# Relative attention on one core: two key tiles in one round of TensorE's tilings, every second tile of maxima scores in full mode

## The chip, the cores and the metric

The kernel runs on one core of one Trainium2 chip. The time is device microseconds of one execution. Before the change three runs took 2206.95, 2209.48 and 2213.20 us; the median is 2209.48 us.

## The reference, cut to what matters

Two layers run over x of shape (2, 1024, 128): attention with rotary positions, a mixture of 8 experts, attention with biases, and a last block of relative attention and 32 experts. The change lies in the relative attention, with 16 heads of 8 columns in each of two batches, so 32 heads in all:

```python
q, k, v = x @ wq, x @ wk, x @ wv                 # 16 heads of 8
p = (pe @ wp).reshape(2 * Ss - 1, H, HD)         # projected relative positions
ac = jnp.einsum('bihd,bjhd->bhij', q, k)
bd_full = jnp.einsum('bihd,phd->bhip', q, p)
rel = jnp.arange(Ss)[:, None] - jnp.arange(Ss)[None, :] + (Ss - 1)
bd = bd_full[:, :, jnp.arange(Ss)[:, None], rel]
att = jax.nn.softmax((ac + bd) * scale, axis=-1)
attn_out = jnp.einsum('bhij,bjhd->bihd', att, v).reshape(Bs, Ss, Ds) @ wo
```

## The kernel before, in words

**A score** is a sum of two products. The content term has 8 columns, split in high and low parts to keep float32 precision: three products stacked on 32 partitions, the *stack* (Qs, Ks). It takes a quarter of TensorE's rows, and Qs and Ks hold it four times, on partitions 0, 32, 64 and 96, so that four of its matmuls can run beside each other ("row stage", `32*128` in the profile). The position term is a full product over 128 partitions: A, made of q and the projected positions, times a fixed table E, each again in high and low parts (Ah, Al in Ahs and Als, Eh, El).

**Two passes per head.** The first finds each query's maximum: for each of 8 query tiles, the stack and Ah x Eh are added in banks 2 and 3 (`stack_scores` L692, `scores` L700), and VectorE takes the negative maximum over 1024 keys (L1144) into M. `max_row` (L733) turns M's 8 columns into rows, ScalarE copies them (L1413), and SP writes them into a row of the stack on two of its four copies (L376), so that the second pass subtracts the maximum. The second pass makes the scores turned, keys on partitions: for each of 8 key tiles kt, the stack (`stack_turned`, L709) and three full products for each half of the queries (`turned`, L715) in banks 0, 1 or 4, 5, in turn; ScalarE takes the exponential (L1426) into PR; `values` (L725) adds PR times V in bank 6, four matmuls in column mode (`128*32`), two passes each. ScalarE copies bank 6 out (L1409).

**A position** is one turn over a head n. Its eight rounds carry the second pass of head n beside the first pass of head n + 2 and the preparation of A of head n + 3 (`prep`, L683: a stack matmul with the weights Ws, in bank 7; VectorE multiplies it by a table, L1139; GpSimd adds, L1622; ScalarE and GpSimd split it in high and low, L1418, L1624). The instructions of each engine stand in the order written by hand; an engine takes them one after the other, and a wait for a semaphore holds back all behind it. Heads 1 to 28 run in a loop of four positions per turn; the heads 0 and 29 to 31 are written out. Ahead of head 0 stands a start, in which the maxima of heads 0 and 1 and the preparations of 0 to 2 are made.

**Slots.** Qs, Ks, Ws, Ahs, Als and M have four slots, head n in slot n mod 4. So head n + 3 goes into the slot of head n - 1. SP, at position n, waits until all 16 halves of turned scores of head n - 1 are done (`st_done`), then issues nine loads for head n + 3: four of Qs and four of Ks (L362), one of Ws (L367). `prep(n + 3, ..., 0)` waits for them (`qk_in`, `ws_in`):

```python
def position(n, s, ahead):                      # SP
    if ahead:
        e.wait_ge(st_done, 1 + 16 * (HB + n))
        load(n + 3, (s + 3) % SLOTS)
    store(n - 1, (s - 1) % SLOTS)
    max_rows(n + 1, (s + 1) % SLOTS)
```

In a round before, TensorE has three parts: row stage (two stack matmuls of the turned scores, two of the maxima scores, in rounds 2 to 5 a preparation), full part (two maxima scores, six turned), values in column mode.

Of the kernel before, what the change touches and what calls it, by code (L numbers as in the profile page):

```python
# [87 lines left out]
def two_layers(nc, A, out):  # L88
    with ExitStack() as ctx:
# [30 lines left out]
        XT = sb("XT", [P, TT * P])  # L120
# [5 lines left out]
        cols = sb("cols", [P, 8])  # L126
# [13 lines left out]
        Ws, Ws_r = two("Ws", [KR, SLOTS, 2 * P])  # L140
# [5 lines left out]
        El = sb("El", [P, L], F32R)  # L146

# [149 lines left out]
        def _(e):  # L297
# [67 lines left out]
            def load_rel(n, s):  # L365
                load_qk(n, s)
                e.dma_start(Ws_r[:, s, :].bitcast(F32), w_stack[bass.ds(n, 1)].rearrange("n r t -> (n r) t")).then_inc(ws_in[s], 16)  # L367
# [150 lines left out]
        def _(e):  # L518
# [153 lines left out]
            def relative_attention():  # L672
                HB = 2 * NH

                def prep(n, s, p, block):

                    if p == 0:
                        e.wait_ge(qk_in[s], 128 * (2 * NH // SLOTS + block + 1))
                        e.wait_ge(ws_in[s], 16 * (block + 1))
                    if p == 0 and not (isinstance(n, int) and n < 3):  # L680
                        e.wait_ge(mt_copied, HB + n - 1)
                    e.wait_ge(prep_mul, 4 * n + p)
                    e.matmul(bank(7), Ws_r[:, s, (p % 2) * P:(p % 2 + 1) * P],  # L683
                             Qs_r[0:KR, s, (p // 2) * GW:(p // 2 + 1) * GW], start=True, stop=True)\
                        .then_inc(prep_ps, 1)

                def stack_scores(n, s, qt, bk=2):

                    e.wait_ge(max_done, 2 + 8 * (HB + n) + qt - (2 if isinstance(n, int) and n < 2 else 0))
                    for kh in range(2):  # L690
                        rows_ = slice((2 + kh) * KR, (3 + kh) * KR)
                        e.matmul(bank(bk + kh), Qs_r[rows_, s, qt * P:(qt + 1) * P],  # L692
                                 Ks_r[rows_, s, kh * GW:(kh + 1) * GW], start=True, stop=False)

                def scores(n, s, qt, bk=2):

                    if qt % 4 == 0:
                        e.wait_ge(prep_split, 2 * n + qt // 4 + 1)
                    for kh in range(2):
                        m = e.matmul(bank(bk + kh), Ahs[s][:, qt * P:(qt + 1) * P], Eh[:, kh * GW:(kh + 1) * GW],  # L700
                                     start=False, stop=True)
                    m.then_inc(s_done, 1)
# [9 lines left out]
                def turned(n, s, kt):  # L712
                    for qh in range(2):
                        for k, (a_part, e_part) in enumerate(((Ahs, El), (Als, Eh), (Ahs, Eh))):
                            m = e.matmul(bank(TURN[kt % 2][qh]), e_part[:, kt * P:(kt + 1) * P],  # L715
                                         a_part[s][:, qh * GW:(qh + 1) * GW], start=False, stop=(k == 2))
                        m.then_inc(st_done, 1)

                def values(n, s, kt):
                    e.wait_ge(exp_done, 2 + 16 * (HB + n) + 2 * kt + 2)  # L720
                    if kt == 0:
                        e.wait_ge(v_ready, HB + n + 1)
                        e.wait_ge(o_copied, HB + n)
                    for g in range(4):
# [37 lines left out]
                for n in range(2):  # L762
                    for half in range(2):
                        for p in range(2 * half, 2 * half + 2):
                            if n == 1 and p == 2:
                                e.wait_ge(mt_copied, HB + 1)
                            prep(n + 1, n + 1, p, 0)
                        for qt in range(4 * half, 4 * half + 4):
                            stack_scores(n, n, qt, FIRST[(QT * n + qt) % 3])
                            scores(n, n, qt, FIRST[(QT * n + qt) % 3])  # L770
                            if n == 1 and qt == 1:
                                max_row(0, 0, 10)
# [6 lines left out]
                values(NH - 1, SLOTS - 1, QT - 1)  # L779
# [139 lines left out]
        def _(e):  # L919
# [212 lines left out]
            def relative_attention():  # L1132
# [152 lines left out]
        def _(e):  # L1285
# [116 lines left out]
            def relative_attention():  # L1402
# [17 lines left out]
                def position(n, s, pairs, first=False, prepare=True, rows_next=True):  # L1420
                    for kt in range(QT):
# [6 lines left out]
                        if kt == 0 and not first:  # L1428
# [3 lines left out]
                        if prepare and kt in (4, 6):  # L1432
                            high(n + 3, (s + 3) % SLOTS, kt // 2 - 2)
# [112 lines left out]
        def _(e):  # L1546
# [13 lines left out]
            def front(f):  # L1560
# [147 lines left out]
    "rope": ([P, 2, L], F32), "w_out": ([P, 3, P], F32), "cols": ([P, 8], F32), "rows": ([P, 3, P], F32),  # L1708
# [6 lines left out]
def layout(i):  # L1715
# [15 lines left out]
                     i["L1_ffn_ln1_g"], i["L1_ffn_ln1_b"], i["L1_ffn_ln2_g"], i["L1_ffn_ln2_b"]], 1)  # L1731
# [41 lines left out]
```

## Time and profile before

| | |
|---|---|
| three runs | 2206.95, 2209.48, 2213.20 us |
| the profiled execution | 2201.49 us, its span 2199.3 us |
| TensorE busy | 2038.2 us, 93% of the span |
| VectorE, ScalarE, GpSimd busy | 1412.8, 1192.4, 519.3 us |
| mean granted clock of TensorE | 0.942 of full speed |
| relative attention, start and end | about 1091 to 1957 us of the span |

A line of the profile is named by the line of the kernel (L715), the engine, the operation, and what it writes and reads. PE is TensorE's matmul, PEld its weight load, DVE VectorE, ACT ScalarE, POOL GpSimd, SPq the queue of SyncE, which issues all DMAs here. "Idle before" is the time for which an engine had nothing to do ahead of an instruction, with what released it. In rows of the timeline several instructions of a line are merged ("x2"); the duration is then from the first one's start to the last one's end. PEclk is the clock granted to TensorE as a share of 2.4 GHz; it has two levels, 1.00 and 0.50.

### The profile page before, as it was taken

The page shows a single profiled execution, that of the slowest core. Times are in us where ns is not written, and L with a number is a line of the kernel's source. Part 1 is how long each engine was busy: PE and PEld are TensorE (multiplying, and loading weights), DVE is VectorE, ACT ScalarE, POOL GpSimd, SP SyncE. Part 2 cuts the span into 40 slices and gives each one's busy share as a digit, 9 for nine tenths or more (in the row PEclk, how much of TensorE's full clock was granted, in tenths as well). Part 3 has the DMA queues.
Part 4 walks back from the last instruction along what each step waited for, and adds up shares of the span by engine and source line. Part 5 has one row for each costly group of instructions (what it writes and reads, how often), then busy time and mean ns, then how long its engine had stood idle before and what let it go on. Part 6 is the DMA issues. An engine that isn't in the chain of part 4 may idle for free.

```text
span 2199.3 us, 42839 instructions
## 1 busy us (share of the span) xinstructions
PE 2038.2 (93%) x13696; PEld 1144.6 (52%) x13696; DVE 1412.8 (64%) x1857; ACT 1192.4 (54%) x2289; POOL 519.3 (24%) x497
## 2 busy tenths in 40 slices
PE   5999999599986999999489999999999999986998
PEld 2344443377762344444245555555555555544887
DVE  6999997556658899996654444444444444325776
ACT  2788888266641888888214444444444444432554
POOL 2000000278861000000222222211222222003664
PEclk8899999699996999999759999999999999987999
DMA  8444442221106444442521111221111112013654
GB/s 274 124 116 112 125 109 73 71 107 59 48 0 178 111 123 108 124 114 75 171 69 46 45 45 44 59 52 45 44 44 44 44 48 59 12 51 129 217 215 145
DMA packets 94607, 202.48 MB, mean 92 GB/s; under 512 B 20368, under 2 KB 53648, under 8 KB 89104
## 3 DMA queue, kind: packets, MB, share of 16 engines
q1 hardware_dynamic: 94544, 201.69, 32.2%
q8 instruction: 33, 0.54, 0.1%
q14 instruction: 30, 0.25, 0.0%
HBM read 166.62 MB, written 36.57 MB: 92 GB/s over the span
## 4 chain that ended last, share of the span: by engine, by line
PE 47%; DVE 2%; SPq 1%; issue 1%; DMA 1%; ACT 0%; POOL 0%; DVEq 0%; POOLq 0%; ACTq 0%
PE PS L715 16%; PE PS L700 8%; PE PS L790 8%; PE PS L725 7%; PE PS L709 5%; PE PS L683 2%; SPq L362 1%; PE PS L692 0%; PE PS L733 0%; DMA Ws_r<-w_stack 0%; SPq L324 0%; DMA rope<-r_dram 0%; PE PS L529 0%; PE PS L550 0%; SPq L335 0%
## 5 line engine op out<-in xcount | busy, mean ns | idle before, releaser
L1123 DVE TENSOR_REDUCE M<-PS 128x1 f32<-128x1024 f32 x512 | 599.0, 1221 | 54.0 <-PE PS L594 54.0
L1388 ACT ACTIVATE PR<-PS 128x512 f32<-128x512 f32 x1024 | 535.0, 589 | 104.8 <-PE PS L614 103.7
L1144 DVE TENSOR_REDUCE M<-PS 128x1 f32<-128x1024 f32 x256 | 313.6, 1225 | 420.4 <-PE PS L700 420.4
L1426 ACT ACTIVATE PR<-PS 128x512 f32<-128x512 f32 x512 | 305.9, 598 | 456.9 <-PE PS L715 450.4
L614 PE MATMUL PS<-Qs_r,Ks_r 32*128 32x512 f32 x1024 | 378.0, 502 | 1.2 <-ACT PR L1388 0.9
L624 PE MATMUL PS<-PR,Va 128*32 128x256 f32 x4096 | 316.3, 393 | 0.0
L594 PE MATMUL PS<-Ks_r,Qs_r 32*128 32x512 f32 x1024 | 266.0, 516 | 16.5 <-DVE M L1123 11.5
L1558 POOL TENSOR_TENSOR Va<-Vt,nil 128x64 f32<-128x64 f32 x96 | 27.8, 293 | 729.9 <-PE PS L624 598.3
L594 PEld LDWEIGHTS PS<-Ks_r,Qs_r 32*128 32x128 f32 x1024 | 98.5, 189 | 194.5 <-issue 123.8
L614 PEld LDWEIGHTS PS<-Qs_r,Ks_r 32*128 32x128 f32 x1024 | 152.3, 183 | 90.7 <-ACT PR L1388 65.0
L1622 POOL TENSOR_TENSOR qk<-rt 128x512 f32<-128x512 f32 x64 | 81.9, 1280 | 357.7 <-DVE rt L1139 357.7
L725 PE MATMUL PS<-PR,Va 128*32 128x256 f32 x2048 | 163.6, 391 | 0.1
L715 PE MATMUL PS<-BIG_r,Eh 128*128 128x512 f32 x512 | 159.3, 392 | 0.0
L624 PEld LDWEIGHTS PS<-PR,Va 128*32 128x32 f32 x4096 | 87.8, 108 | 122.4 <-ACT PR L1388 70.7
L1648 POOL TENSOR_TENSOR BIG_r<-BIG,BIG_r 128x512 fp32r<-128x512 f32 (+1 forms) x96 | 129.9, 1361 | 32.6 <-ACT BIG_r L1456 32.6
L692 PE MATMUL PS<-Ks_r,Qs_r 32*128 32x512 f32 x512 | 132.7, 513 | 0.0
L709 PE MATMUL PS<-Qs_r,Ks_r 32*128 32x512 f32 x512 | 128.3, 497 | 1.3 <-DVE M L1144 1.3
L1201 DVE TENSOR_TENSOR BIG<-PS,SRC 128x512 f32<-128x512 f32 (+1 forms) x96 | 66.0, 688 | 79.7 <-PE PS L790 75.7
L790 PE MATMUL PS<-BIG_r,PR_r 128*128 128x512 f32 x384 | 109.4, 394 | 3.4 <-POOL BIG_r L1686 3.4
L790 PE MATMUL PS<-Ah,PR_r 128*128 128x512 f32 x352 | 110.0, 394 | 0.0
L715 PEld LDWEIGHTS PS<-BIG_r,Eh 128*128 128x128 f32 x512 | 96.1, 188 | 21.4
L700 PE MATMUL PS<-Eh,Ah 128*128 128x512 f32 x256 | 102.1, 483 | 0.0
(184 smaller groups left out, 3008.1 us busy)
## 6 DMA issues: line engine op xcount, KB each, us to landing
Qs_r<-q_stack SPq DMA_DIRECT2D x384, 128.0 KB, 2.6
Ks_r<-k_stack SPq DMA_DIRECT2D x384, 128.0 KB, 3.1
Qs<-g_dram SPq DMA_DIRECT2D x30, 1024.0 KB, 4.9
o_dram<-Ob SPq DMA_DIRECT2D x96, 128.0 KB, 2.6
Ks<-g_dram SPq DMA_DIRECT2D x10, 1024.0 KB, 4.8
q_stack<-hl SPq DMA_DIRECT2D x18, 256.0 KB, 3.3
k_stack<-hl SPq DMA_DIRECT2D x18, 256.0 KB, 3.9
q_stack<-PR_r SPq DMA_DIRECT2D x18, 256.0 KB, 3.7
```

The costliest lines, as they stand in the source:

```text
L594: m = e.matmul(bank(2 + 2 * (qt % 2) + kh), Qs_r[rows_, s, qt * P:(qt + 1) * P], Ks_r[rows_, s, kh * GW:(kh + 1) * GW], start=True, stop=True)
L614: e.matmul(bank(RING[(x if x < 4 else x + 1) % 3]), Ks_r[rows_, s, kt * P:(kt + 1) * P], Qs_r[rows_, s, qh * GW:(qh + 1) * GW], start=True ...
L624: m = e.matmul(PS[32 * g:32 * g + VC, 6, 0:256], Va[:, s, kt, :], PR[:, kt % 4, g * 256:(g + 1) * 256], start=(kt == 0), stop=(kt == QT - 1))
L700: m = e.matmul(bank(bk + kh), Ahs[s][:, qt * P:(qt + 1) * P], Eh[:, kh * GW:(kh + 1) * GW], start=False, stop=True)
L709: e.matmul(bank(TURN[kt % 2][qh]), Ks_r[rows_, s, kt * P:(kt + 1) * P], Qs_r[rows_, s, qh * GW:(qh + 1) * GW], start=True, stop=False)
L715: m = e.matmul(bank(TURN[kt % 2][qh]), e_part[:, kt * P:(kt + 1) * P], a_part[s][:, qh * GW:(qh + 1) * GW], start=False, stop=(k == 2))
L725: m = e.matmul(PS[32 * g:32 * g + VC, 6, 0:256], Va[:, s, kt, :], PR[:, kt % 4, g * 256:(g + 1) * 256], start=(kt == 0), stop=(kt == QT - 1))
L790: m = e.matmul(out, w[a], h[b], start=start and n == 0, stop=n == 2 or not start, skip_group_check=not start)
L1123: e.tensor_reduce(M[:, s, qt:qt + 1], PS[:, 2 + 2 * (qt % 2):4 + 2 * (qt % 2), :] .rearrange("p a b -> p (a b)"), AX.X, ALU.max, negate=Tr ...
L1144: e.tensor_reduce(M[:, s, qt:qt + 1], PS[:, bk:bk + 2, :].rearrange("p a b -> p (a b)"), AX.X, ALU.max, negate=True).then_inc(max_done, 1)
L1388: e.activation(PR[:, kt % 4, qh * GW:(qh + 1) * GW], bank(RING[(x if x < 4 else x + 1) % 3]), ACT.Exp, scale=SCALE).then_inc(exp_done, 1)
L1426: e.activation(PR[:, kt % 4, qh * GW:(qh + 1) * GW], bank(TURN[kt % 2][qh]), ACT.Exp)\
```

## The change

- **Rounds.** A position has four rounds in place of eight, each with two key tiles kt and kt + 1. The row stage holds the stack matmuls of the turned scores of both tiles, those of the maxima scores of tile kt, and one preparation. Then come, in full mode, the two scores of kt, the turned scores of kt, the first half of those of kt + 1, the maxima scores of kt + 1, and the second half of the turned ones. Then the values of two tiles, kt - 2 and kt - 1.
- **Fourfold scores.** The maxima scores of an odd tile (`scores4`) use no row stage: the four copies of the stack are taken as one product over 128 partitions, which gives four times the content term, and Ah is multiplied by E4 = 4 x Eh, kept in the first 1024 columns of XT (GpSimd makes it with two additions). The maximum comes out fourfold, and the copy of the maxima's row scales odd tiles by 0.25, with a ninth column of cols. At the start, all 16 tiles of heads 0 and 1 are made so.
- **Preparations.** They stand in rounds 0 to 3 of the four, one in each, where they stood in rounds 2 to 5 of the eight, and use partitions 64 to 95 (Ws is loaded there) in place of 0 to 31. On VectorE each stands ahead of the round's two maxima.
- **Maxima's row.** It is written in the unused half of bank 6, the values' bank, in place of bank 7, between the halves of the turned scores in round 1; it waits for the evacuation of head n - 1, and the first values of a head wait for its copy.
- **ScalarE.** The evacuation of head n - 1 stands behind the exponentials of tile 1 in place of tile 0; the second split into the high part behind tile 7 in place of tile 6.

SP's order and its waits are the same as before.

The next rows are TensorE's, in the loop, before: the last part of round 1 with the maxima's row (L733), and round 2, whose row stage ends with the first preparation (L683) of head n + 3. L709 is the turned stack, L692 and L700 the maxima scores, L715 the turned scores.

```order
L733 MATMUL PS<-ident,M 8x128 [waits prep_mul]
L707 REGISTER_ALU
L709 MATMUL PS<-Qs_r,Ks_r 128x512 [waits exp_done] x2
L689 REGISTER_ALU
L692 MATMUL PS<-Ks_r,Qs_r 128x512 [waits max_done]
L692 MATMUL PS<-Ks_r,Qs_r 128x512
L678 ISA
L679 ISA [waits qk_in0]
L683 MATMUL PS<-Qs_r,Ws_r 128x512 [waits prep_mul,mt_copied,ws_in0]
L700 MATMUL PS<-Eh,BIG_r 128x512 x2
L715 MATMUL PS<-Ah,El 128x512
```

The same preparation now, TensorE, from the beginning of the loop's first position: L720 is the turned stack, L692 and L700 the maxima scores of the even tile, L725 the turned scores.

```order
L718 ISA [waits m_in1]
L720 MATMUL PS<-Qs_r,Ks_r 128x512 [waits exp_done] x2
L689 ISA
L692 MATMUL PS<-Ks_r,Qs_r 128x512 [waits max_done]
L692 MATMUL PS<-Ks_r,Qs_r 128x512
L718 REGISTER_ALU
L720 MATMUL PS<-Qs_r,Ks_r 128x512 [waits exp_done]
L718 REGISTER_ALU
L720 MATMUL PS<-Qs_r,Ks_r 128x512 [waits exp_done]
L680 ISA
L681 ISA [waits qk_in0]
L682 ISA [waits ws_in0]
```

The wait for the loads (`qk_in0`, `ws_in0`) stood in the third round of the position and stands in the first row stage now. The preparation's matmul follows the last of these rows; all full matmuls of the round stand behind it.

The end of that round, TensorE, now: L711 are the fourfold scores, L725 the turned scores, L736 the values.

```order
L706 REGISTER_ALU
L711 MATMUL PS<-Ks_r,Qs_r 128x512 [waits max_done]
L711 MATMUL PS<-Ks_r,Qs_r 128x512
L711 MATMUL PS<-XT_r,BIG_r 128x512 x2
L725 MATMUL PS<-Ah,El 128x512
L725 MATMUL PS<-Al,Eh 128x512
L725 MATMUL PS<-Ah,Eh 128x512
L730 ISA
L736 MATMUL PS<-PR,Va 32x256 [waits exp_done]
L736 MATMUL PS<-PR,Va 32x256 x3
```

The odd tile's four score matmuls have moved from a row stage and a full part of their own into the full part that is there; the values follow once for two tiles.

The diff, cut to its core:

```diff
+        E4 = XT_r[:, 0:L]
@@ SP
-                e.dma_start(Ws_r[:, s, :].bitcast(F32), w_stack[...])
+                e.dma_start(Ws_r[WROW, s, :].bitcast(F32), w_stack[...])
@@ TensorE, prep
-                    if p == 0 and not (isinstance(n, int) and n < 3):
-                        e.wait_ge(mt_copied, HB + n - 1)
                     e.wait_ge(prep_mul, 4 * n + p)
-                    e.matmul(bank(7), Ws_r[:, s, (p % 2) * P:(p % 2 + 1) * P],
-                             Qs_r[0:KR, s, (p // 2) * GW:(p // 2 + 1) * GW], start=True, stop=True)\
+                    e.matmul(bank(7), Ws_r[WROW, s, (p % 2) * P:(p % 2 + 1) * P],
+                             Qs_r[WROW, s, (p // 2) * GW:(p // 2 + 1) * GW], start=True, stop=True)\
...
+                def scores4(n, s, qt, bk, before):
+
+                    e.wait_ge(max_done, 2 + 8 * (HB + n) + qt - before)
+                    if qt % 4 == 0:
+                        e.wait_ge(prep_split, 2 * n + qt // 4 + 1)
+                    for q, k, first in ((Qs_r[:, s, :], Ks_r[:, s, :], True), (Ahs[s], E4, False)):
+                        for kh in range(2):
+                            m = e.matmul(bank(bk + kh), q[:, qt * P:(qt + 1) * P], k[:, kh * GW:(kh + 1) * GW],
+                                         start=first, stop=not first)
+                    m.then_inc(s_done, 1)
...
-                def max_row(n, s, preps):
+                def max_row(n, s, copied):
 
                     e.wait_ge(max_done, 2 + 8 * (HB + n) + 8)
-                    e.wait_ge(prep_mul, preps)
-                    e.matmul(PS[0:QT, 7, 0:P], M[:, s, :], ident[:], start=True, stop=True).then_inc(mt_done, 1)
+                    e.wait_ge(o_copied, HB + copied)
+                    e.matmul(PS[0:QT, 6, 256:256 + P], M[:, s, :], ident[:], start=True, stop=True,
+                             skip_group_check=True).then_inc(mt_done, 1)
@@ TensorE, position
-                    for kt in range(QT):
+                    for c in range(QT // 2):
+                        kt = 2 * c
                         stack_turned(n, s, kt)
                         if ahead:
                             stack_scores(n + 2, s2, kt)
-                        if prepare and 2 <= kt < 6:
-                            prep(n + 3, s3, kt - 2, block + (s >= 1))
+                        stack_turned(n, s, kt + 1)
+                        if prepare:
+                            prep(n + 3, s3, c, block + (s >= 1))
                         if ahead:
                             scores(n + 2, s2, kt)
-                        turned(n, s, kt)
-                        if kt == 0:
-                            if not first:
-                                values(n - 1, (s - 1) % SLOTS, QT - 1)
-                        else:
-                            values(n, s, kt - 1)
-                        if kt == 1 and rows_next:
-                            max_row(n + 1, (s + 1) % SLOTS, 4 * (n + 3) if prepare else 4 * NH)
+                        turned(n, s, kt, 0)
+                        if c == 1 and rows_next:
+                            max_row(n + 1, (s + 1) % SLOTS, n)
+                        turned(n, s, kt, 1)
+                        turned(n, s, kt + 1, 0)
+                        if ahead:
+                            scores4(n + 2, s2, kt + 1, 2, 0)
+                        turned(n, s, kt + 1, 1)
+                        for k in range(kt - 2, kt):
+                            if k >= 0:
+                                values(n, s, k, rows_next)
+                            elif not first:
+                                values(n - 1, (s - 1) % SLOTS, QT + k)
@@ VectorE, position
-                    for kt in range(QT):
+                    for c in range(QT // 2):
+                        if prepare:
+                            prep(n + 3, (s + 3) % SLOTS, c)
                         if ahead:
-                            row_max(n + 2, (s + 2) % SLOTS, kt)
-                        if prepare and 2 <= kt < 6:
-                            prep(n + 3, (s + 3) % SLOTS, kt - 2)
+                            row_max(n + 2, (s + 2) % SLOTS, 2 * c)
+                            row_max(n + 2, (s + 2) % SLOTS, 2 * c + 1)
@@ ScalarE
-                    e.activation(MT[:, s, :], PS[0:QT, 7, 0:P], ACT.Copy).then_inc(mt_copied, 1)
+                    scale = 0.25 if isinstance(n, int) and n < 2 else cols[0:QT, 8:9]
+                    e.activation(MT[:, s, :], PS[0:QT, 6, 256:256 + P], ACT.Identity, scale=scale).then_inc(mt_copied, 1)
...
-                        if kt == 0 and not first:
+                        if kt == 1 and not first:
                             evacuate(n - 1, (s - 1) % SLOTS, pairs)
...
-                        if prepare and kt in (4, 6):
-                            high(n + 3, (s + 3) % SLOTS, kt // 2 - 2)
+                        if prepare and kt in (4, 7):
+                            high(n + 3, (s + 3) % SLOTS, int(kt == 7))
@@ GpSimd
+                    own(e.tensor_tensor(E4, Eh[:].bitcast(F32), Eh[:].bitcast(F32), ALU.add))
+                    own.settle()
+                    own(e.tensor_tensor(E4, E4.bitcast(F32), E4.bitcast(F32), ALU.add))
```

## Rows read from the trace of the kernel before

**Rows 1.** Windows of the loop: PE, PEld, DVE, ACT, POOL busy, PEclk, DMA, GB/s
```profile
1170.00:1873.00 703.00, 700.58 (x4524) 404.33 (x4523) 330.83 (x327) 306.34 (x546) 147.25 (x136) 1.00 0.19 48
```
**Rows 2.** The page's groups: maxima and exponentials; busy, mean ns, idle before
```profile
L1144 DVE TENSOR_REDUCE M<-PS 128x1 f32<-128x1024 f32 x256 | 313.6, 1225 | 420.4 <-PE PS L700 420.4
L1426 ACT ACTIVATE PR<-PS 128x512 f32<-128x512 f32 x512 | 305.9, 598 | 456.9 <-PE PS L715 450.4
```
**Rows 3.** Waits from 1150 to 1900 us: total us, times, longest
```profile
PEld PS L683 <- DMA Ks_r<-k_stack: 0.4, 1, 0.4
```
**Rows 4.** Timeline of SP's queue: start us, duration
```profile
1322.23 1.72 SPq L362 DMA_DIRECT2D Qs_r<-q_stack  x4
...
1326.06 0.32 SPq L367 DMA_DIRECT2D Ws_r<-w_stack  x1
```
**Rows 5.** Timeline of TensorE, end of a position and its next round
```profile
1321.41 0.63 PE L715 MATMUL PS<-BIG_r,Eh 128*128 128x512 f32 x2
...
1322.54 0.50 PE L709 MATMUL PS<-Qs_r,Ks_r 32*128 32x512 f32 x2
...
1322.97 0.73 PE L700 MATMUL PS<-Eh,Ah 128*128 128x512 f32 x2
...
1323.54 0.39 PE L715 MATMUL PS<-BIG_r,El 128*128 128x512 f32 x1
...
1324.44 0.61 PE L715 MATMUL PS<-BIG_r,Eh 128*128 128x512 f32 x2
...
1324.99 0.64 PE L725 MATMUL PS<-PR,Va 128*32 128x256 f32 x8
...
1325.56 0.50 PE L709 MATMUL PS<-Qs_r,Ks_r 32*128 32x512 f32 x2
```
**Rows 6.** Timeline of TensorE, a row stage with a preparation
```profile
1306.58 0.49 PE L709 MATMUL PS<-Qs_r,Ks_r 32*128 32x512 f32 x2
...
1306.92 0.39 PE L683 MATMUL PS<-Qs_r,Ws_r 32*128 32x512 f32 x1
1307.24 0.73 PE L700 MATMUL PS<-Eh,Ah 128*128 128x512 f32 x2
```
**Rows 7.** Timeline of TensorE, values of two tiles in the earlier attention
```profile
1036.23 1.07 PE L624 MATMUL PS<-PR,Va 128*32 128x256 f32 x16
```
**Rows 8.** Timeline of TensorE, values, maxima's row, next row stage
```profile
1328.04 0.64 PE L725 MATMUL PS<-PR,Va 128*32 128x256 f32 x8
...
1328.80 0.50 PE L709 MATMUL PS<-Qs_r,Ks_r 32*128 32x512 f32 x2
```
**Rows 9.** The line of Ws loads: ns min/median/max, first and last start; landing
```profile
L367 SPq DMA_DIRECT2D Ws_r<-w_stack x23: 315/316/319, 1171.2 to 1739.0; - x23
...
DMA to landing us min/median/max: 2.4/2.8/3.0
```
**Rows 10.** Windows round idle gaps and the stage's start, columns as rows 1
```profile
673.30:677.95 4.65, 0.03 (x2) 0.01 (x1) 4.04 (x19) 1.36 (x3) 2.55 (x2) 0.86 0.75 243
677.95:683.50 5.55, 4.51 (x8) 2.21 (x9) 5.07 (x21) 0.98 (x2) 0.00 (x0) 0.50 0.41 127
1072.60:1079.40 6.80, 4.88 (x15) 3.45 (x16) 3.45 (x8) 0.78 (x1) 0.00 (x0) 0.50 0.36 102
1103.00:1141.00 38.00, 32.97 (x77) 13.54 (x77) 24.24 (x24) 4.07 (x6) 10.89 (x11) 0.50 0.26 78
```
**Rows 11.** Timeline of TensorE, a tile at the start
```profile
1105.01 0.79 PE L692 MATMUL PS<-Ks_r,Qs_r 32*128 32x512 f32 x2
1105.74 1.22 PE L700 MATMUL PS<-Eh,Ah 128*128 128x512 f32 x2
1106.89 0.79 PE L692 MATMUL PS<-Ks_r,Qs_r 32*128 32x512 f32 x2
```
**Rows 12.** Timeline of GpSimd ahead of the stage
```profile
1051.71 2.34 POOL L1578 TENSOR_TENSOR El<-PR,Eh 128x1024 fp32r<-128x1024 f32 x1
...
1060.29 1.27 POOL L1567 TENSOR_TENSOR X<-X,SRC 128x512 f32<-128x512 f32 x1 [5.02 <-DVE SRC L943]
```

More of the change, by code:

```diff
@@ L119, in two_layers @@
         SRC = sb("SRC", [P, TT, P])
-        XT = sb("XT", [P, TT * P])
+        XT, XT_r = two("XT", [P, TT * P])
         ident = sb("ident", [P, P])
@@ L125, in two_layers @@
         rel = sb("rel", [P, 2, L])
-        cols = sb("cols", [P, 8])
+        cols = sb("cols", [P, 9])
         rows = sb("rows", [P, 3, P])
@@ L138, in two_layers @@
         Ob = sb("Ob", [P, 2, 256])
-        Ws, Ws_r = two("Ws", [KR, SLOTS, 2 * P])
+        Ws, Ws_r = two("Ws", [P, SLOTS, 2 * P])
+        WROW = slice(2 * KR, 3 * KR)
         Ah = sb("Ah", [P, 2, L], F32R)
@@ L366, in load_rel @@
                 load_qk(n, s)
-                e.dma_start(Ws_r[:, s, :].bitcast(F32), w_stack[bass.ds(n, 1)].rearrange("n r t -> (n r) t")).then_inc(ws_in[s], 16)
+                e.dma_start(Ws_r[WROW, s, :].bitcast(F32), w_stack[bass.ds(n, 1)].rearrange("n r t -> (n r) t")).then_inc(ws_in[s], 16)
             def attention(a):
@@ L679, in prep, with stack_scores, scores @@
                         e.wait_ge(ws_in[s], 16 * (block + 1))
-                    if p == 0 and not (isinstance(n, int) and n < 3):
-                        e.wait_ge(mt_copied, HB + n - 1)
                     e.wait_ge(prep_mul, 4 * n + p)
-                    e.matmul(bank(7), Ws_r[:, s, (p % 2) * P:(p % 2 + 1) * P],
-                             Qs_r[0:KR, s, (p // 2) * GW:(p // 2 + 1) * GW], start=True, stop=True)\
+                    e.matmul(bank(7), Ws_r[WROW, s, (p % 2) * P:(p % 2 + 1) * P],
+                             Qs_r[WROW, s, (p // 2) * GW:(p // 2 + 1) * GW], start=True, stop=True)\
                         .then_inc(prep_ps, 1)
-                def stack_scores(n, s, qt, bk=2):
-                    e.wait_ge(max_done, 2 + 8 * (HB + n) + qt - (2 if isinstance(n, int) and n < 2 else 0))
+                def stack_scores(n, s, qt):
+                    e.wait_ge(max_done, 2 + 8 * (HB + n) + qt)
                     for kh in range(2):
                         rows_ = slice((2 + kh) * KR, (3 + kh) * KR)
-                        e.matmul(bank(bk + kh), Qs_r[rows_, s, qt * P:(qt + 1) * P],
+                        e.matmul(bank(2 + kh), Qs_r[rows_, s, qt * P:(qt + 1) * P],
                                  Ks_r[rows_, s, kh * GW:(kh + 1) * GW], start=True, stop=False)
-                def scores(n, s, qt, bk=2):
+                def scores(n, s, qt):
                     if qt % 4 == 0:
@@ L699, in scores @@
                     for kh in range(2):
-                        m = e.matmul(bank(bk + kh), Ahs[s][:, qt * P:(qt + 1) * P], Eh[:, kh * GW:(kh + 1) * GW],
+                        m = e.matmul(bank(2 + kh), Ahs[s][:, qt * P:(qt + 1) * P], Eh[:, kh * GW:(kh + 1) * GW],
                                      start=False, stop=True)
+                    m.then_inc(s_done, 1)
[7 more added lines that the diff above has]
+                                         start=first, stop=not first)
                     m.then_inc(s_done, 1)
@@ L710, in stack_turned, with turned, values @@
                                  Qs_r[rows_, s, qh * GW:(qh + 1) * GW], start=True, stop=False)
[L712 to L719, printed above, removed]
+                def turned(n, s, kt, qh):
+                    for k, (a_part, e_part) in enumerate(((Ahs, El), (Als, Eh), (Ahs, Eh))):
+                        m = e.matmul(bank(TURN[kt % 2][qh]), e_part[:, kt * P:(kt + 1) * P],
+                                     a_part[s][:, qh * GW:(qh + 1) * GW], start=False, stop=(k == 2))
+                    m.then_inc(st_done, 1)
+                def values(n, s, kt, rows_next=True):
                     e.wait_ge(exp_done, 2 + 16 * (HB + n) + 2 * kt + 2)
@@ L764, in relative_attention @@
                         for p in range(2 * half, 2 * half + 2):
-                            if n == 1 and p == 2:
-                                e.wait_ge(mt_copied, HB + 1)
                             prep(n + 1, n + 1, p, 0)
                         for qt in range(4 * half, 4 * half + 4):
-                            stack_scores(n, n, qt, FIRST[(QT * n + qt) % 3])
-                            scores(n, n, qt, FIRST[(QT * n + qt) % 3])
+                            scores4(n, n, qt, FIRST[(QT * n + qt) % 3], 2)
                             if n == 1 and qt == 1:
-                                max_row(0, 0, 10)
+                                max_row(0, 0, 0)
                 position(0, 0, 0, first=True)
@@ L778, in relative_attention @@
                     position(NH - SLOTS + s, NH // SLOTS - 1, s, ahead=s < 2, prepare=False, rows_next=s < 3)
-                values(NH - 1, SLOTS - 1, QT - 1)
+                for kt in range(QT - 2, QT):
+                    values(NH - 1, SLOTS - 1, kt)
             def zero_acc(k):
@@ L1707 @@
     "x": ([TT * P, P], F32), "ident": ([P, P], F32), "w_qkv": ([P, 3, 5 * P], F32),
-    "rope": ([P, 2, L], F32), "w_out": ([P, 3, P], F32), "cols": ([P, 8], F32), "rows": ([P, 3, P], F32),
+    "rope": ([P, 2, L], F32), "w_out": ([P, 3, P], F32), "cols": ([P, 9], F32), "rows": ([P, 3, P], F32),
     "rel": ([P, 3, L], F32), "w_rt0": ([P, 8], F32), "w_rt1": ([P, NE1], F32),
```

5 lines of the change are left out of this document (4 added, 1 removed).

## The prediction

> **What bounds the kernel now.** I read the windows first. Over 703 us of relative attention's loop TensorE is busy 700.58 of 703.00 us and the granted clock is 1.00, the 2.4 GHz level [rows 1]. VectorE and ScalarE wait there for TensorE: the maxima (1,225 ns each) sat idle 420.4 us ahead of them, the exponentials (598 ns) 456.9 us, nearly all released by TensorE [rows 2]. Of the waits on TensorE's side one bears on this change: once in the stage a weight load of the preparation (L683) waited for a transfer, for 0.4 us [rows 3]. So a position costs what TensorE's order costs. The loads of Ws, one to a position, are issued from 1171.2 to 1739.0 us, 23 of them [rows 9]: 22 steps of 25.81 us. I have to price that order and then look for what it newly waits for.
>
> **A round before.** A round without preparation runs from row stage to row stage, 1322.54 to 1325.56: 3.02 us [rows 5]. It splits into row stage to first full matmul 0.43, eight full matmuls to the values 2.02, values to the next row stage 0.57. With a preparation the row stage takes 1306.58 to 1307.24, 0.66, so its second layer adds 0.23; the preparation starts 0.34 after the stage does, and the full part 0.32 after it [rows 6]. Full matmuls stand 0.225 apart (1323.54 to 1324.44 is four steps, 0.90) [rows 5]. Check: four rounds at 3.02, four at 3.25 and the row of maxima give 25.3; the trace has 25.8; the 0.5 left lies round the maxima row, whose copy the first preparation waits for.
>
> **The new round of two key tiles, nothing waiting.** The row stage has two layers now (the second tile's stack matmuls use the row groups of the first, the preparation stands beside them on a third): 0.66. The full part has 2 scores, 12 turned and 4 fourfold scores, 18 matmuls: 2.02 + 10 x 0.225 = 4.27. The values of two tiles: 0.57 for the first, and 0.43 for the second (in the earlier attention sixteen value passes take 1.07 against 0.64 for eight [rows 5, 7]): 1.00. Sum 5.93, against 6.04 for two plain rounds and 6.50 for two with preparation. The 0.45 us of the two extra full matmuls nearly eats the saved switches; what is left is the preparation, which lies beside other work. The row of maxima cost 0.76 - 0.57 = 0.19 beside the values [rows 5, 8]. In the midst of the full run it needs a way in (0.32, the full-to-values step), a second pass (0.11, half of a 0.22 us value pass of twice its columns) and a way back to full: 0.5 us; bounds 0.2, the old price, and 1.0, twice my value. A position costs 4 x 5.93 + 0.5 = 24.2, a gain of 1.6 if nothing waits.
>
> **What it newly waits for.** Preparation 0 of head n + 3 is the first use of the slot that SP reloads. SP starts that reload when the last turned matmul of head n - 1 has ended; the change leaves that alone. Before, the preparation stood in the third round; now it stands at the end of the first row stage, and behind it in TensorE's order stand all scores and turned matmuls of the round. From the rows: the last turned pair begins at 1321.41 and ends at 1322.04; the first load is issued at 1322.23, the ninth (Ws) at 1326.06 [rows 4, 5]; Ws lands 2.8 us after its issue (2.4 to 3.0) [rows 9], at 1328.86, and with 0.1 allowed for the signal the matmul can run: 1328.96, 6.9 us after the end of the last turned matmul. It would be reached at 1322.54 + 0.43 (second values) + 0.34 = 1323.31. **TensorE waits 5.6 us in every one of the 28 inner positions.** Before, it got there at about 1329.4 and the cushion was half a microsecond, which is why the one wait of 0.4 us shows. What that preparation waited for the copy of the maxima's row goes with it; the new round is priced without it. Nothing covers the new wait: ScalarE has one tile's exponentials left, VectorE's first product waits for the same matmul, and two maxima stand behind it.
>
> The position is now a ring: start of the last turned matmul (0.40 before its end, so 1321.64) to the preparation 7.3 us (1328.96 - 1321.64); preparation to full 0.32; 18 full matmuls, first to last start, 4.27 - 0.32 = 3.95; three whole rounds 17.79; maxima 0.5. Sum 29.86 us, 4.05 over the 25.81 before.
>
> **The clock.** Idle gaps of this size lower it. TensorE had nothing to do from 673.3 to 677.95, the clock fell within the gap and stood at 0.50, the 1.2 GHz level, for the 5.55 us after it; after another gap it stood there for 6.80 us, from 1072.6 on [rows 10]. Behind those gaps TensorE was 81% and 72% busy; here a full run of 18 matmuls follows, so I take 5 us at the low level. Half the work of that time is lost: 2.5 us per position (bounds 0, if the wait does not lower it, and 3.4, half of 6.80). A position is 32.36 us, 6.55 more than before; 28 of them: **+183.4 us**.
>
> The Trainium skill has this case in "TensorE: Matmul & The Clock Gate", section "HAM oscillation — how this bites in real kernels": a loop that waits for a transfer in each turn loses the warm clock in each turn, and the page counts the slow restart as a cost of its own beside the wait. By a reading without that rule the sum would be 28 x 4.05 = 113 us, with it 183; this trace agrees with the rule at its two gaps.
>
> **The rest.** The first position has no such wait (its slot is loaded long before): -1.6. Head 29 has no preparation: 4 x 5.93 + 0.5 against 8 x 3.02 + 0.2, nothing. Heads 30 and 31 have no scores: a round before is 3.02 less two full matmuls, 2.57; two now are 0.66 + 12 full (2.02 + 4 x 0.225 = 2.92) + 1.00 = 4.58 against 5.14, eight times: -4.5. The 16 tiles at the start run at the low level, 1.88 each [rows 11]; four full matmuls take there about 4 x 0.45 = 1.80, twice the 0.225 each: -1.3, and up to -9 if the clock rises and VectorE's 1.23 becomes the bound; I take -3. The two extra additions that make E4 take about 2.34 each on GpSimd (as the split of the same width), ahead of a task before which it sat idle for 5.02 [rows 12]: hidden; without that cover +4.7 once. Moving the evacuation behind the second tile, Identity with a scale in place of Copy, and the copy of maxima in bank 6 lie in ScalarE's idle time: nothing. The last fourfold score starts three steps before the round's last turned matmul and takes 0.39 [rows 5], so the maximum of an odd tile ends 1.0 us after that matmul starts (-0.68 + 0.39 + 1.23, and a little); its banks are wanted at 0.32 + 1.00 = 1.3: no wait, 0.3 us of cushion. Sum -9.1.
>
> Total 2201.49 + 183.4 - 9.1 = 2375.8 for an execution like the profiled one; the median of the runs is 8.0 above that one (2209.48): **2384 us**.
>
> **Rivals.** *The wait is there, the clock stays up* (10%): 2201.5 + 113.4 - 9.1 + 8 = 2314. Against it both gaps; for it only that they stood in another stage. *The loads land sooner* (5%): if the landing, 2.8 us in a busy queue, and the issue (3.83 for eight) together shrink by 2 us, 28 x 2 = 56 less: 2328. The landing's 2.4 to 3.0 speaks against it. *The clock does not recover* (3%): from 1103.0 to 1141.0 it stood at 0.50 with TensorE 87% busy [rows 10], and if all 22.6 us of work in a position ran so, each would take 50 us: about 2870. In that stretch the row stage took 0.73 of the 1.88 us of a tile [rows 11]; once full runs began at 1141.0, 3.2 us were enough, and it was at 1.00 for the 703 us of rows 1. *The other side, faster* (4%): the mechanism is the cheaper order, its place each double round, its price 1.6 us for each of 29 positions, and the 4.5 and 3 of the ends: 2209.5 - 46.4 - 7.5 = 2156. It decides only if Ws is in within 1.3 us of the last turned matmul's end, and the loads alone are issued over 3.83 us; I would have to have misread which load the preparation waits for.
>
> My forecast holds 78%. Its own range is 2350 to 2410 (clock loss 1.7 to 3.4 us per position, landing +-0.3, maxima row 0.2 to 1.0). The range takes in the two cases just below it: 2310 to 2410. A difference under 0.3%, 7 us, could not be told from no change here. Faster 4%, the same 1%, slower 95%.
>
> **What would show it.** In the changed profile: a wait of PE L683 for Ks_r or Ws_r, 28 times, 5 to 6 us each, some 157 us in sum; TensorE's busy share in the stage falling from 99.7% to about 83%; the granted clock there near 0.9; loads of Ws 32.4 us apart; from the preparation's matmul in the first round to the next last turned matmul 22.6 us plus the clock's part; the second values 0.43 behind the first. Wrong if Ws loads are under 28 us apart, if L683 waits under 4 us, or if a maximum or an exponential becomes the releaser in every round.

## The result and the profile after

The changed kernel takes 2393.51 us (median of 4 runs, 2383.25 to 2397.54) against 2208.22: ratio 1.0827, 95% interval 1.0799 to 1.0856. It is slower, 9.5 us over my 2384 and inside the range. The profiled execution took 2397.54 us, span 2395.0.

Windows over the loop of relative attention, heads 1 to 28 (columns as [rows 1]: PE, PEld, DVE, ACT, POOL busy, granted clock, DMA):

```profile
1184.00:2063.00 879.00, 738.52 (x4482) 482.30 (x4482) 334.56 (x324) 300.40 (x540) 146.06 (x135) 0.89 0.14 37
```

TensorE, which was busy 99.7% there [rows 1], is busy 84%, and its clock has fallen from 1.00 to 0.89. The waits, 1150 to 2110 us (total us, times, longest), say for what; [rows 3] had a single 0.4 us:

```profile
PE PS L683 <- DMA Ws_r<-w_stack: 149.8, 28, 6.3
```

28 times, once per position of the loop, 5.35 us each of idle time. The line of the Ws loads gives the length of a position, as [rows 9] did:

```profile
L369 SPq DMA_DIRECT2D Ws_r<-w_stack x28: 315/316/319, 1181.4 to 2063.0; - x28
```

27 steps in 881.6 us: 32.65 us each, against 25.81. One boundary between two positions in the timeline, the counterpart of [rows 4 to 6]:

```profile
1502.57 0.63 PE L725 MATMUL PS<-BIG_r,Eh 128*128 128x512 f32 x2
...
1503.13 1.07 PE L736 MATMUL PS<-PR,Va 128*32 128x256 f32 x16
...
1503.39 1.72 SPq L364 DMA_DIRECT2D Qs_r<-q_stack  x4
...
1504.47 0.39 PE L720 MATMUL PS<-Qs_r,Ks_r 32*128 32x512 f32 x2
...
1507.21 0.32 SPq L369 DMA_DIRECT2D Ws_r<-w_stack  x1
...
1510.19 0.79 PE L683 MATMUL PS<-Qs_r,Ws_r 32*128 32x512 f32 x1 [5.33 <-DMA Ws_r<-w_stack]
...
1510.91 1.22 PE L700 MATMUL PS<-Eh,Ah 128*128 128x512 f32 x2
```

The last turned pair ends at 1503.20, SP issues its first load 0.19 later, the ninth at 1507.21. TensorE ends its row stage at 1504.86 and the preparation runs at 1510.19, 7.0 us after the last turned matmul ended. In a round without a wait it starts 0.34 us after the row stage does, before that stage's last matmuls have ended [rows 6]; here that would be 1504.47, so it comes 5.7 us late, 5.3 of them idle. The pair of scores behind it takes 1.22 us in place of 0.73: the clock is low. Two more windows round this wait:

```profile
1506.80:1517.00 10.20, 6.81 (x15) 5.07 (x16) 1.91 (x2) 1.79 (x3) 0.00 (x0) 0.50 0.20 45
1517.00:1540.80 23.80, 21.36 (x152) 13.36 (x150) 10.48 (x10) 9.33 (x17) 5.42 (x5) 1.00 0.13 37
```

The low level, 1.2 GHz, stood here from 1506.8 to 1517.0; 6.8 us of it lay behind the wait. This is one of four positions with 10.2 us at the low level; in the other 24 of the loop it lasted 6.8 us.

The bookkeeping of the two profiled executions, 195.7 us of span apart, by landmarks on TensorE: loop +184.7 (881.6 against 696.9); the start of the stage, first preparation to first turned stack, -8.4 (40.8 against 49.2); the first position -1.6; what follows the last Ws load up to the last values +2.9 (it holds the 28th wait, and the last heads' gain); the last stage -2.1; and +20.2 ahead of the stage, where the kernels are the same but for E4. Of these, 8.1 lie in the second attention (330.8 against 322.7 us), 7.1 up to the end of the first one and 0.6 between the two; in the other kernels below the second attention took 322.7 to 331, so that is scatter between executions. 4.4 lie in the front, from the last values of the second attention to the first preparation; some 3 of them are the change's, see the last experiment.

### The profile page after: what moved, and what is told of

It reads as the page before. It is cut to its first block, busy times and chain, and to the rows that moved or that the text cites. A ratio compares the mean times of both kernels' runs of the same rounds, so it can differ in the third digit from the quotient of the medians.

```text
span 2395.0 us, 42868 instructions
## 1 busy us (share of the span) xinstructions
PE 2080.6 (87%) x13696; PEld 1237.2 (52%) x13696; DVE 1420.3 (59%) x1857; ACT 1190.1 (50%) x2289; POOL 521.3 (22%) x499
## 4 chain that ended last, share of the span: by engine, by line
PE 42%; SPq 5%; DMA 4%; DVE 2%; issue 2%; ACT 0%; POOL 0%; DVEq 0%; POOLq 0%; ACTq 0%
PE PS L725 17%; PE PS L807 7%; PE PS L711 5%; PE PS L736 4%; SPq L364 4%; PE PS L700 4%; DMA Ws_r<-w_stack 3%; PE PS L720 3%; PE PS L683 1%; DVE M L1161 0%; PE PS L744 0%; SPq L326 0%; DMA rope<-r_dram 0%; PE PS L531 0%; PE PS L552 0%
## 5 line engine op out<-in xcount | busy, mean ns | idle before, releaser
L616 PE MATMUL PS<-Qs_r,Ks_r 32*128 32x512 f32 x1024 | 381.2, 512 | 1.9 <-ACT PR L1406 1.4
L626 PE MATMUL PS<-PR,Va 128*32 128x256 f32 x4096 | 325.5, 403 | 0.0
L596 PE MATMUL PS<-Ks_r,Qs_r 32*128 32x512 f32 x1024 | 269.6, 524 | 16.9 <-DVE M L1140 11.2
L1156 DVE TENSOR_TENSOR rt<-PS,rel 128x512 f32<-128x512 f32 x128 | 88.5, 691 | 319.4 <-PE PS L683 317.9
L683 PE MATMUL PS<-Qs_r,Ws_r 32*128 32x512 f32 x128 | 63.4, 496 | 162.7 <-DMA Ws_r<-w_stack 152.6
L725 PE MATMUL PS<-BIG_r,Eh 128*128 128x512 f32 x512 | 173.8, 423 | 0.0
L736 PE MATMUL PS<-PR,Va 128*32 128x256 f32 x2048 | 136.8, 385 | 0.0
L725 PEld LDWEIGHTS PS<-BIG_r,Eh 128*128 128x128 f32 x512 | 106.3, 208 | 24.9
L683 PEld LDWEIGHTS PS<-Qs_r,Ws_r 32*128 32x128 f32 x128 | 26.7, 209 | 178.9 <-issue 162.9
L725 PE MATMUL PS<-BIG_r,El 128*128 128x512 f32 x256 | 111.5, 436 | 0.0
```

The source lines that it names most:

```text
L596: m = e.matmul(bank(2 + 2 * (qt % 2) + kh), Qs_r[rows_, s, qt * P:(qt + 1) * P], Ks_r[rows_, s, kh * GW:(kh + 1) * GW], start=True, stop=True)
L616: e.matmul(bank(RING[(x if x < 4 else x + 1) % 3]), Ks_r[rows_, s, kt * P:(kt + 1) * P], Qs_r[rows_, s, qh * GW:(qh + 1) * GW], start=True ...
```

## Experiments

The theory: the reload of a slot, needed at the front of the position since the change, costs TensorE a wait and low clock behind it, and the new order is faster than the old where nothing waits. The rivals: the new rounds or the fourfold scores are slow in themselves; or the low clock costs nothing beyond the wait.

**Preparations later, all else as changed.** Round c = 0 takes the last preparation of the head before (TensorE's part of the edit; VectorE and ScalarE follow the same order):

```diff
-                        if prepare:
-                            prep(n + 3, s3, c, block + (s >= 1))
+                        if c == 0:
+                            if ahead and not first:
+                                prep(n + 2, s2, 3, 0)
+                        elif prepare:
+                            prep(n + 3, s3, c - 1, block + (s >= 1))
```

> The changed kernel with one thing moved: preparations 0 to 2 of head n + 3 stand in rounds 1 to 3 of position n, and preparation 3 in round 0 of position n + 1 (so that a round still has one); everything else of the change stays. Theory (the wait for the reloaded slot, and the low clock behind it, cost 28 x 7.9 us and the new rounds themselves save): the loads are in 7.4 us after the last turned matmul starts, the preparation is reached at 7.6, so no wait; a position takes 24.2 to 24.4 us, Ws loads 24.3 apart, TensorE's clock 1.00 in the loop, the time about 2157 us (2145 to 2170). Rival (the fourfold scores, the two-layer row stage or the maxima's row in bank 6 are slow in themselves): the time stays over 2209 us.

Measured: 2169.33 us, ratio 0.9812 (0.979 to 0.9833), faster than before by 1.9%, at the upper edge of my 2145 to 2170. The loop's windows and its Ws loads:

```profile
1169.50:1833.60 664.10, 664.10 (x4479) 436.25 (x4478) 331.75 (x324) 296.47 (x539) 147.20 (x135) 1.00 0.19 50
L369 SPq DMA_DIRECT2D Ws_r<-w_stack x28: 315/316/318, 1169.5 to 1833.7; - x28
```

No wait, clock 1.00, 24.60 us per position. So the place of the first preparation turned a gain of 1.2 us per position into a loss of 6.8. My 24.2 was 0.4 short.

**The same place alone, in the kernel before** (TensorE's part of the edit):

```diff
-                    if p == 0 and not (isinstance(n, int) and n < 3):
-                        e.wait_ge(mt_copied, HB + n - 1)
+                    if p in (0, 2) and not (isinstance(n, int) and n < 3):
+                        e.wait_ge(mt_copied, HB + n - 2 + p // 2)
...
-                        if prepare and 2 <= kt < 6:
-                            prep(n + 3, s3, kt - 2, block + (s >= 1))
+                        if prepare and kt < 4:
+                            prep(n + 3, s3, kt, block + (s >= 1))
```

> The kernel before with one thing moved: the four preparations of a head in rounds 0 to 3 in place of 2 to 5 (with the waits for bank 7 that this needs), none of the other edits. Theory (the place of the first preparation alone makes the loss): the preparation is reached 1.2 us after the last turned matmul starts and the loads are in at 7.4, a wait of 6.1 us less the 0.5 round the maxima's row, and 2.5 for the low clock: 28 x 8.3 = 232 us over before, about 2440 us. Rival (the rounds of two tiles or the fourfold scores make it): about 2209 us.

Measured: 2443.44 us, ratio 1.1062 (1.1007 to 1.1117). The waits, 1150 to 2110 us:

```profile
PE PS L683 <- DMA Ks_r<-k_stack: 126.3, 21, 6.3
PE PS L683 <- DMA Ws_r<-w_stack: 41.7, 7, 6.1
```

28 waits, 6.0 us each, the clock at 0.90 in the loop, 34.15 us per position. Neither rounds of two tiles nor fourfold scores are in this kernel; the loss needs neither.

**The order kept, the reload earlier.** SP waits for the last stack matmuls of head n - 1:

```diff
-                        e.wait_ge(st_done, 1 + 16 * (HB + n))
+                        if a == 2:
+                            e.wait_ge(stk_done, 2 * n)
...
+                        if kt == QT - 1:
+                            m.then_inc(stk_done, 1)
```

> The changed kernel with its order kept, and the reload of a slot started when the last stack matmuls of head n - 1's turned scores are done (a semaphore of their own) in place of the last turned matmul. Those end about 3.9 us before the last turned matmul starts, so Ws is in at about 3.0 us after it and the preparation is reached at 1.65. Theory: the wait shrinks from 5.3 to about 1.35 us, the clock stays at 1.00 in the loop, a position takes 25.6 us, the time about 2195 us (2180 to 2215). Rival (only the length of the wait counts, the clock stays low): 2393 less 28 x 4 = 2281 us. Rival (the order, not the wait): 2393.

Measured: 2214.47 us, ratio 1.0019 (1.0001 to 1.0037). The waits, 1160 to 1900 us, and windows in the loop's second half:

```profile
PE PS L687 <- DMA Ws_r<-w_stack: 30.4, 28, 1.8
```
```profile
1450.00:1876.00 426.00, 409.70 (x2709) 266.66 (x2708) 200.09 (x196) 182.38 (x328) 89.12 (x82) 1.00 0.18 47
```

The idle time is 1.1 us per position and the clock mostly stays up; in the first eleven positions it still fell five times, for 3.4 us each. 179 us are back without an instruction of TensorE's moved. But my 25.6 us per position was too low, and with it the time of 2195:

```profile
L370 SPq DMA_DIRECT2D Ws_r<-w_stack x28: 315/316/318, 1162.3 to 1876.6; - x28
```
```profile
1512.39 0.50 PE L724 MATMUL PS<-Qs_r,Ks_r 32*128 32x512 f32 x2
...
1514.30 0.49 PE L687 MATMUL PS<-Qs_r,Ws_r 32*128 32x512 f32 x1 [1.18 <-DMA Ws_r<-w_stack]
```

27 steps in 714.3 us: 26.5 us each, and 26.1 in the second half, where the clock no longer fell; before it was 25.81. The preparation starts 1.91 us after its row stage in place of 0.34, so it is 1.57 late where 1.18 show as idle. With about 1.5 us lost per position, the order's gain of 1.2 is more than eaten, and the loop is 17 us longer than before. The start of the stage (39.7 us against 49.2) and the positions outside the loop gave most of that back, which is why the whole time is the same as before.

**Both.** Diff: the two above together.

> e1_prep_late and e2_load_early together. Theory: in e1_prep_late the loads are just in time (7.4 against 7.6 us), so starting them 4.3 us sooner changes nothing: within 0.3% of e1_prep_late. Rival: e1_prep_late still waits in some positions: this one is faster by 28 times that wait.

Measured: 2168.20 us, ratio 0.9788 (0.9767 to 0.9809), the loop 664.2 us, as in the first experiment to 0.1 us. There the loads came in time in every position.

**The wait filled with work.** Matmuls whose result is overwritten, ahead of the wait for the slot:

```diff
+                    if p == 0 and not isinstance(n, int):
+                        e.wait_ge(prep_mul, 4 * n + p)
+                        for _ in range(20):
+                            e.matmul(bank(7), Eh[:, 0:P], Eh[:, 0:GW], start=True, stop=True)
```

> The changed kernel with 20 full matmuls (128 x 128 weights, 512 columns, of the table Eh, into bank 7, their result overwritten) ahead of the wait for the slot in each of the 28 loop positions: work of about 4.5 us laid into the wait of 5.3 us. The outputs are the same. Theory (the clock's fall is a cost of its own): the loads arrive as before, TensorE's clock stays at 1.00 in the loop, a position falls from 32.66 to about 30.1 us, the time from 2393 to about 2323 us, although more work is done. Rival (the low clock only fills time that would be waited anyway): 2393 us, no change.

Measured: 2376.17 us, ratio 1.0753 (1.0696 to 1.0809), a miss by 53 us. Most positions took 29.6 to 32.5 us, near the 30.1 expected, but at the start of each turn of the loop (four positions), the first excepted, two gaps appeared on TensorE, and the clock fell with them; the position that holds them took 36.5 to 38.3 us:

```profile
1426.27 0.50 PE L724 MATMUL PS<-Qs_r,Ks_r 32*128 32x512 f32 x2 [2.63 <-issue]
1429.70 0.79 PE L696 MATMUL PS<-Ks_r,Qs_r 32*128 32x512 f32 x2 [2.93 <-issue]
```

TensorE waits for nothing that the profile shows ("issue"), and the page's instruction queue has grown from 33 packets to

```profile
q8 instruction: 88, 1.44, 0.3%
```

I took it that the longer loop body was fetched anew in each turn, and made the same work with fewer instructions, 5 float32 matmuls, which are ten in the trace (`e.matmul(bank(7), ident[:], rel[:, 0, 0:GW])`); that is half the instructions of the first filling, not the quarter of my expectation.

> The changed kernel with the wait filled by 5 float32 matmuls (a quarter of e3_fill's instructions for about the same 4.4 us of work; their result is overwritten). e3_fill took 30.2 us in three of four positions and 37 in the fourth, where each turn of the loop begins, with 88 instruction packets in place of 33. Theory (the longer body of the loop had to be fetched in each turn, and without that the clock's gain shows): all positions at about 30.2 us, 33 packets, the clock 1.00, the time about 2323 us. Rival (what cost time there comes with the fill itself, not with the number of instructions): every fourth position again at 37 us, 2376 us.

Measured: 2333.21 us, ratio 1.0575 (1.0543 to 1.0608). The queue and the loop up to 1650 us:

```profile
q8 instruction: 43, 0.70, 0.1%
```
```profile
1200.00:1650.00 450.00, 439.04 (x2613) 269.93 (x2612) 183.53 (x180) 165.60 (x298) 79.89 (x74) 1.00 0.15 39
```

26 of 27 steps took 29.8 to 31.4 us, one 37.7, with the same two gaps (1651.41 to 1654.08 and 1654.87 to 1657.52). The same queue by windows: no packet from 1300 to 1645 us, and from 1646 to 1660

```profile
q8 instruction: 4, 0.07, 1.7%
```

In the changed kernel it has none from 1300 to 2090 us; with the longer filling it has some in every turn. Gaps and packets stand at the same place in time. So 4.56 us of useless work per position (28 of them, 128 us) made the kernel 60 us faster than the changed one, since the clock stays at 1.00 but for that one place. The low clock is a cost of its own: 32.65 - 30.2, 2.4 us per position.

**Fourfold scores alone, in the kernel before.** Odd tiles of heads 2 to 31 by `scores4`, the rounds as they were:

```diff
-                        if ahead:
+                        if ahead and kt % 2 == 0:
                             stack_scores(n + 2, s2, kt)
...
-                            scores(n + 2, s2, kt)
+                            if kt % 2:
+                                scores4(n + 2, s2, kt, 2)
+                            else:
+                                scores(n + 2, s2, kt)
```

> The kernel before, rounds of one tile, with the fourfold scores for the odd tiles of heads 2 to 31 alone (their stack matmuls leave the row stage, where they ran beside the turned ones, and come as two more full matmuls). Theory (two full matmuls cost 0.45 us and a row stage with two in place of four matmuls is no shorter): 4 x 0.45 = 1.8 us per position, 30 positions, and 3 us for E4: 2209 + 57 = 2266 us. Rival (the row stage shortens as its matmuls are halved): 0.45 - 0.2 per odd tile, 2242 us. Rival (fourfold scores are free): 2209 us.

Measured: 2269.48 us, ratio 1.0271 (1.0244 to 1.0298). A position takes 27.71 us (1186.2 to 1934.4 for 27 steps), 1.90 more. The row stage of an odd tile with a preparation:

```profile
1504.36 0.50 PE L719 MATMUL PS<-Qs_r,Ks_r 32*128 32x512 f32 x2
1504.70 0.39 PE L684 MATMUL PS<-Qs_r,Ws_r 32*128 32x512 f32 x1
1505.03 0.73 PE L710 MATMUL PS<-Ks_r,Qs_r 128*128 128x512 f32 x2
```

0.67 us with two stack matmuls in its first layer, as with four [rows 6]. The fourfold scores are a price, 0.47 us per odd tile, that the merged rounds have to pay back; with them a position takes 24.60 us.

**The maxima's row back in bank 7, beside the values,** on top of the first experiment (TensorE's part; its copy by ScalarE stands behind the exponentials of tile 3, and preparation 1 waits for it):

```diff
-                        if c == 1 and rows_next:
-                            max_row(n + 1, (s + 1) % SLOTS, n)
...
+                        if c == 1 and rows_next:
+                            max_row(n + 1, (s + 1) % SLOTS, 4 * (n + 3) + 1 if prepare else 4 * NH)
```

> e1_prep_late with the maxima's row back in bank 7, between the last turned matmul and the values of round 1, its copy on ScalarE behind the exponentials of tile 3, and preparation 1 waiting for that copy. In the changed kernel the row in the midst of the full run costs 0.52 us; beside the values it cost 0.19. Theory: 31 x 0.33 = 10 us less than e1_prep_late, about 2147 us. Rival: the copy is late for preparation 1 (it is wanted 1.9 us after the last turned matmul starts and done at 1.5 by my reckoning) and the wait eats the gain: the same time as e1_prep_late.

Measured: 2153.26 us, ratio 0.9718 (0.9695 to 0.9741), a position 24.26 us, 0.34 less than 24.60, 9 us over the loop; the other 7 us against the first experiment lie outside it. In the changed kernel the row stood so, in the midst of the full run:

```profile
1520.53 0.61 PE L725 MATMUL PS<-BIG_r,Eh 128*128 128x512 f32 x2
...
1521.07 0.39 PE L744 MATMUL PS<-ident,M 128*8 128x128 f32 x2
...
1521.73 0.62 PE L725 MATMUL PS<-BIG_r,Eh 128*128 128x512 f32 x2
```

From the second matmul of the first pair (1520.76) to 1521.73 are 0.97 us, for two steps of 0.225: the row costs 0.52, near the 0.5 forecast.

**The table made elsewhere,** on top of that one: Eh and E4 by ScalarE, El by GpSimd, all at the start of relative attention.

```diff
+                e.activation(Eh[:], PR[:, 3, :], ACT.Copy).then_inc(e4_ok, 1)
+                e.activation(E4, PR[:, 3, :], ACT.Copy, scale=4.0).then_inc(e4_ok, 1)
```

> e5_row_bank7 with the table's parts made elsewhere: Eh and E4 by ScalarE at the start of relative attention, El by GpSimd there, none of it on GpSimd during the front before. In the traces VectorE's four normalising instructions of that front take 5.48 us in the kernel before and 7.93 in e1_prep_late, beside GpSimd's table work, and 1.12 where GpSimd is idle. Theory (GpSimd's work slows VectorE there, and my forecast of the two E4 additions as hidden was wrong): the four take 1.1 us, the front shortens by 6 to 8 us against e5_row_bank7, the time is about 2146 us. Rival (VectorE waits there for something else): the four still take over 5 us and the time is that of e5_row_bank7.

VectorE and GpSimd in the first experiment, where the additions for E4 are the two of XT_r:

```profile
1055.01 1.89 POOL L1585 TENSOR_TENSOR Eh<-PR,nil 128x1024 fp32r<-128x1024 f32 x1 [44.82 <-DMA PR<-in_rel]
...
1055.42 7.93 DVE L963 TENSOR_SCALAR xn<-SRC,mv,sd 128x128 f32<-128x128 f32 x4
1056.98 1.89 POOL L1605 TENSOR_TENSOR XT_r<-Eh 128x1024 fp32r<-128x1024 f32 x1
1058.95 1.89 POOL L1607 TENSOR_TENSOR XT_r<-XT_r 128x1024 fp32r<-128x1024 f32 x1
1060.92 2.34 POOL L1609 TENSOR_TENSOR El<-PR,Eh 128x1024 fp32r<-128x1024 f32 x1
```

and the same four of VectorE with the table gone from there:

```profile
1064.16 1.11 DVE L967 TENSOR_SCALAR xn<-SRC,mv,sd 128x128 f32<-128x128 f32 x4
```

Four instructions that take 1.11 us alone took 7.93 beside GpSimd's work, and TensorE waited for them in the first experiment:

```profile
1063.40 1.11 PE L531 MATMUL PS<-ident,xn 128*128 128x128 f32 x4 [12.71 <-DVE xn L963]
```

That is the Trainium skill's rule in "SBUF — State Buffer", section "Who interferes with whom": VectorE and GpSimd share a pair of ports that one holds at a time, and tensor_scalar may use it. The trace agrees, with 7.93 us against 1.11. The front, from the last values of the second attention to the first preparation, shortened from 54.1 to 46.7 us. The whole time did not show it: 2152.48 us, ratio 0.9727 (0.9702 to 0.9753), against 2153.26. The start of the stage became 2.5 us longer, and the other 5 us are within the scatter of runs (2144.74 to 2155.46 here, 2144.68 to 2162.28 there); the expected 2146 us is neither met nor refuted.

## Why the prediction was right, and where it was off

- **The wait.** Forecast 5.6 us, 28 times, 157 in sum. My 5.6 ran from the point where the preparation would be reached without a wait; on these terms it measures 5.72 (1504.47 to 1510.19). The profile counts idle time, which begins 0.39 later, when the last stack matmuls end: 5.35, 28 times, 149.8. I had equated the two. The three terms (signal 0.19, issue 3.82, landing 2.8) were those of before. The fourth, the allowance for the signal, was 0.1 and measures 0.18 (1507.21 + 2.8 to 1510.19). Moving the preparation alone into the kernel before gave 2443 us; I expected 2440 of that run.
- **The clock.** Forecast 2.5 us per position; the filled wait measures 2.4. I had taken 5 us at the low level behind each wait, from two gaps elsewhere. By the trace's clock records it began within the wait in all 28 positions, and 3.4 to 6.8 us of it, 5.0 on average, lay behind. The rival in which the clock stays up is refuted.
- **The new round.** Forecast 5.93 us. It measures 6.0 in the changed kernel: the row stages of rounds 2 and 3 start at 1525.60 and 1531.59. Steps of full matmuls with 0.23 between them, not 0.225, make most of it. With the row of maxima a position is 24.6, not 24.2. So the order gains 1.2 us, not 1.6. This and the 0.08 above are why 32.36 became 32.65, 8 us over the loop.
- **The start.** Forecast -3, measured -8.4, near my bound of -9, which was for a clock that rises there. It did. The granted clock was 1.00 from 1134.7 on; before, it was low until 1144.3.
- **E4.** Forecast as hidden in GpSimd's idle time. This step failed: the additions, 1.89 us each, stretched VectorE's normalising instructions beside them, and TensorE waited for those. The front took 53.8 us in place of 49.4, and 52.3 to 54.6 in the other six kernels with E4's additions there and the new rounds, and 53.1 in the one with old rounds; without them 49.4 and 50.6. On average that is 3.3 us. The last experiment took all of the table's work away from there, so E4's own share rests on this comparison of fronts. I had looked for who waits for GpSimd, and not for who shares something with it.
- **The sum.** Part of its closeness is luck. The start came out 5.4 us under the forecast, the loop 8 us and E4 some 3 us over it. The profiled execution, 2397.54 us, is 21.7 over the 2375.8 forecast for it, 15.8 of them scatter in the stages ahead; the kernel before had been profiled in an execution 8.0 us under its median, the changed one in the slowest of its four.

## What to carry to other kernels

When an instruction moves forward in an in-order stream, find the first use of every reloaded buffer in what moves, and add up the chain from the last reader of the old contents: signal, all issues of the queue, landing. Here it was 7 us, and the same edit with the first use one round later was a gain of 1.9%. Price an idle gap of TensorE twice, once for its length and once for the clock behind it. Ask of idle time on GpSimd also what VectorE does meanwhile.

## What I had not expected of the hardware

- GpSimd's additions of 128 x 1024 float32 stretched four VectorE instructions from 1.11 to 7.93 us; even the kernel before lost 4.4 us so (5.48 us for the same four).
- A loop body longer by 160 TensorE instructions (matmuls and weight loads) showed two gaps of 2.4 to 3.2 us in each turn but the first, and 88 instruction packets in place of 33. That the fetch makes the gaps is my reading: packets and gaps came and went together in two kernels, and in the second at the same place in time. Why the shorter filling shows them in one turn alone stays open.
- Work that is thrown away made a kernel faster, 2333 against 2393 us, by keeping the clock up.
- The second attention, the same in all kernels, took 322.7 to 331 us from one execution to another. What makes that stays open.
